# Who waits for the ring to come free: GpSimd itself instead of SyncE, in a graph kernel that gathers edges through a ring of buffers

## The reference, cut to what matters

```python
def _L0_gnn_ref(x, edge_index, edge_type, W_rel, W_root, bias):   # 3 layers, 8 edge types, D = 256
    src, dst = (edge_index[0], edge_index[1])
    for l in range(n_layers):
        xr = jnp.einsum('nd,rde->rne', x, W_rel[l])
        msg = xr[edge_type, src]
        agg = jax.ops.segment_sum(msg, dst, num_segments=x.shape[0])
        x = jax.nn.relu(agg + x @ W_root[l] + bias[l])
    return x

def _L1_gnn_ref(x, Wv, bv, wq, bq, wk, bk, src, dst):
    h = x @ Wv + bv
    q = h @ wq + bq
    k = h @ wk + bk
    e = q[src] + k[dst]
    c = jnp.where(e > 0, e, NEG_SLOPE * e)
    m = jax.ops.segment_max(c, dst, num_segments=n)
    ex = jnp.exp(c - m[dst])
    s = jax.ops.segment_sum(ex, dst, num_segments=n)
    attn = ex / s[dst]
    msg = h[src] * attn[:, None]
    return jax.ops.segment_sum(msg, dst, num_segments=n)

h = jnp.maximum(_layernorm(x, axis=-1), 0.0)
x = x + _L0_gnn_ref(h, ...)
h = jnp.maximum(_layernorm(x, axis=-1), 0.0)
x = x + _L1_gnn_ref(h, ...)
```

## Time and profile before

| | us |
|---|---|
| median of 3 runs | 5318.29 |
| lowest and highest of them | 5300.09, 5330.71 |
| the profiled execution's own time | 5230.69 |
| its span, first to last instruction | 5229.0 |
| GpSimd busy | 3053.6 (58%) |
| TensorE busy | 3608.1 (69%) |
| ScalarE busy | 2196.4 (42%) |
| VectorE busy | 1656.7 (32%) |

### The profile page before, as it was taken

The page is one execution under the profiler, slowest core; times in us unless marked ns, Lnnn a source line. Parts: engine busy times, 40 slices in busy tenths (PEclk is TensorE's granted clock), DMA queues, the critical chain, the costliest instruction groups (busy, mean ns, idle before and its releaser), DMA issues.

```text
span 5229.0 us, 56297 instructions
## 1 busy us (share of the span) xinstructions
PE 3608.1 (69%) x12674; PEld 2495.8 (48%) x12674; DVE 1656.7 (32%) x4423; ACT 2196.4 (42%) x6033; POOL 3053.6 (58%) x3302
## 2 busy tenths in 40 slices
PE   9986787777874877777775554544554666666667
PEld 4444554555552554545553343433433555545555
DVE  4533343333331222212221111111112545445444
ACT  2232443334442443433442333333333666556665
POOL 1145666666654666666664666666664566556664
PEclk9997888889887988888887677767766888888888
DMA  6553555555553444444443333333332333333332
GB/s 215 194 197 125 185 185 173 180 185 183 183 178 110 132 138 129 134 130 140 131 136 101 97 104 102 102 103 104 103 101 76 96 101 102 94 88 101 100 98 76
DMA packets 240051, 681.47 MB, mean 130 GB/s; under 512 B 60188, under 2 KB 111988, under 8 KB 215028
## 3 DMA queue, kind: packets, MB, share of 16 engines
q0 software_dynamic: 152400, 419.03, 27.6%
q10 hardware_dynamic: 57240, 186.43, 9.6%
q1 hardware_dynamic: 30092, 72.34, 3.8%
HBM read 501.99 MB, written 175.58 MB: 130 GB/s over the span
## 4 chain that ended last, share of the span: by engine, by line
PE 41%; another core or an unknown queue 26%; issue 14%; ACT 12%; DVE 6%; ACTq 1%; DVEq 0%; DMA 0%; SPq 0%
PE bank L1549 16%; PE sum_ps L1635 13%; PE sum_ps L1762 5%; ACT masks L1454 4%; ACT masks L1360 3%; PE bank L1718 2%; PE bank L1712 2%; DVE root L812 2%; PE turn_ps L1534 1%; ACT wide L1431 1%; ACT masks L1368 1%; PE sum_ps L1628 1%; ACT stage L1470 1%; ACT stage L1267 1%
## 5 line engine op out<-in xcount | busy, mean ns | idle before, releaser
L594 POOL DMA_INDIRECT ring<-table,code x2361 | 2236.4, 947 | 1377.8 <-issue 730.6
L1635 PE MATMUL sum_ps<-ring,masks 128*128 x5292 | 1445.6, 429 | 310.9 <-issue 295.6
L1635 PEld LDWEIGHTS sum_ps<-ring,masks 128*128 128x128 f32 x5292 | 1134.0, 218 | 587.6 <-issue 407.5
L1549 PE MATMUL bank<-wide,xT 128*128 128x512 f32 (+1 forms) x2744 | 1123.8, 563 | 4.1 <-issue 2.7
L594 POOL DMA_INDIRECT ring<-h_table,code x787 | 744.9, 946 | 503.1 <-SPq L734 254.8
L1360 ACT ACTIVATE masks<-node_row,local 128x128 f32<-128x128 f32 x2646 | 788.0, 387 | 24.8 <-issue 10.8
L1549 PEld LDWEIGHTS bank<-wide,xT 128*128 128x128 f32 x2744 | 514.3, 190 | 560.0 <-issue 548.7
L1762 PE MATMUL sum_ps<-ring,stage 128*128 x1764 | 541.7, 459 | 235.4 <-ACT stage L1470 151.2
L1258 ACT ACTIVATE xT<-turn_ps 128x256 f32<-128x256 f32 x196 | 75.5, 385 | 1441.8 <-remote 594.4
L1762 PEld LDWEIGHTS sum_ps<-ring,stage 128*128 128x128 f32 x1764 | 390.8, 235 | 314.6 <-issue 256.6
L1267 ACT COPY stage<-bank 128x512 f32<-128x512 f32 x441 | 244.3, 584 | 695.6 <-remote 429.2
(11 more groups left out here) (218 smaller groups left out, 2328.3 us busy)
## 6 DMA issues: line engine op xcount, KB each, us to landing
table<-stage ACTq DMA_DIRECT2D x96, 1024.0 KB
back<-table ACTq DMA_DIRECT2D x49, 1024.0 KB
table<-stage SPq DMA_DIRECT2D x48, 1024.0 KB
ring<-table,code POOLq DMA_INDIRECT x2361
ring<-h_table,code POOLq DMA_INDIRECT x787
h_table<-stage ACTq DMA_DIRECT2D x49, 130.0 KB
back<-h_table ACTq DMA_DIRECT2D x49, 130.0 KB
features<-xT SPq DMA_DIRECT2D x49, 128.0 KB, 4.0
```

The costliest lines, as they stand in the source:

```text
L594: pool.indirect_dma_start(slot(c % RING, width), None, table, bass.IndirectOffsetOnAxis(ap=code[:, c:c + 1], axis=0)).then_inc(landed[n % ...
L1549: last = nc.tensor.matmul(bank[q][:, 0:width], xT[:, b, k, :], weights[:, k, 512 * q:512 * q + width], start=(k == 0), stop=(k == K - 1))
L1635: last = nc.tensor.matmul(sum_ps[b][:, 0:D], masks[:, b, s, :], at_offset(slots[s]), start=(s == 0 and l > 0), stop=(s == SLOTS - 1))
```

## The change

GpSimd no longer waits for `released`. It loads the numbers of `need` itself, eight at a time, does the two register steps for each group, and waits for `added` with that value. SyncE only waits for landed groups and counts them in `in_order`. The semaphore `released` and the constants `LAG` and `RELEASES` are gone. What GpSimd waits for is the same count of pieces as before, for the same group, ten before the one that it fills.

```diff
-    LAG = 8
-    RELEASES = GROUPS - RINGS
-    BATCH = 16
+    BATCH = 8
-        released = sem("released")
             def gather_pass(l, table, width):
                 if l:
                     pool.wait_ge(in_order, l * GROUPS)
+                counts = []
                 for n in range(GROUPS):
-                    if n >= RINGS:
-                        pool.wait_ge(released, l * RELEASES + n - RINGS + 1)
+                    m = n - RINGS
+                    if m >= 0:
+                        if m % BATCH == 0:
+                            end = min(m + BATCH, GROUPS)
+                            _, counts = nc.values_load_multi_w_load_instructions(
+                                need[0:1, m:end], engines=[pool.engine], min_val=1, max_val=NT * PIECES,
+                                skip_runtime_bounds_check_because="counts of pieces, largest over the tiles")
+                        value = (counts[m % BATCH] & AT_MOST_PIECES) + (CREDIT + l * NT * PIECES)
+                        settle(pool, value)
+                        pool.wait_ge(added, value)
                     for c in chunks_of(n):
                         pool.indirect_dma_start(
             def relay(l):
-                counts = []
                 for n in range(GROUPS):
                     sp.wait_ge(landed[n % RINGS], 16 * gathers_to(l, n))
                     sp.sem_inc(in_order, 1)
-                    m = n - LAG
-                    if 0 <= m < RELEASES:
-                        if m % BATCH == 0:
-                            end = min(m + BATCH, GROUPS)
-                            _, counts = nc.values_load_multi_w_load_instructions(
-                                need[0:1, m:end], engines=[sp.engine], min_val=1, max_val=NT * PIECES,
-                                skip_runtime_bounds_check_because="counts of pieces, largest over the tiles")
-                        value = (counts[m % BATCH] & AT_MOST_PIECES) + (CREDIT + l * NT * PIECES)
-                        settle(sp, value)
-                        sp.wait_ge(added, value)
-                        sp.sem_inc(released, 1)
```

More of the change, by code:

```diff
@@ L71, in gnn_program @@
     assert PIECES == -(-SLOTS // GROUP)
-    assert (SLOTS + GROUP - 2) // GROUP + 1 <= LAG < RINGS and PIECES >= 3
+    assert (SLOTS + GROUP - 2) // GROUP + 1 < RINGS and PIECES >= 3
     assert 1 < KM and FIRST_BLOCKS * P <= 512
```

## The result

| | before | after |
|---|---|---|
| median, us | 5309.19 | 5442.13 |
| lowest and highest, us | 5242.52, 5330.71 | 5437.61, 5444.87 |
| profiled execution, us (span) | 5230.69 (5229.0) | 5439.88 (5438.2) |

The changed kernel is slower: 1.0324 times the kernel before, 95% interval 1.028 to 1.0367. The medians are 133 us apart and the two profiled executions 209 us, because the profiled execution of the kernel before is shorter than all four runs behind its median.

A forecast was written before the change was run, and what follows sets the result against it. The prediction took GpSimd's own gather pace, 1.25 us each, plus ring stalls ended by TensorE's count, as the bound. Its terms, -8 + 0 + 0 + 0 + 0 = -8 us, gave 5318 - 8 = 5310 us, range 5235 to 5405.

The forecast's parts named there:

- The median: Whole kernel: the time before, 5318 us, on which the forecast laid its sum to reach 5310 us.
- One hop less: Ring stalls on GpSimd: without SyncE's step each ends sooner, 0.028 x 282 = 8 us gained, at most 73 us.
- Landing order and `in_order` sooner: SyncE's queue: releases no longer behind landings, landed counts no longer behind piece waits; 0 each, at most some 5 and 2.3 us.
- Loads and steps: GpSimd's queue: 166 us of loads and 55 us of register steps, hidden behind gathers or inside stalls, costed at 0.
- Rival A: GpSimd's loads and steps stand bare outside stalls: 137 us slower, 5455 us; all 221 us, 5539, if stalls don't shrink; chance 0.13.
- B: GpSimd in the passes: only long loads stick out past the gathers, 75 us slower, 5393 us; chance 0.11.
- C: GpSimd's ring stalls end sooner, the whole 0.26 us of each of 282 going: 73 us faster, 5245 us; chance 0.17.
- Gathers 1.25 us apart across loads: Sign of being right: GpSimd's gathers still start each 1.25 us across loads and steps.
- Time at the ring near 814 us: Sign of being right: GpSimd's ring wait stays near 814 us, now charged to TensorE's sums.
- Pass windows within 10 us: Sign of being right: the windows of the four passes stay within 10 us of before.
- The last sentence on what would make it wrong: Ring stalls: if their count arrives at another point of the gathers, everything forecast is small beside a large number.

The follow-up runs named there:

- e9: Kernel before, but GpSimd waits for `added` against constants, without relay, loads or registers; run at the slow level: 0.9994 of the kernel before.
- e5: The changed kernel once more, unaltered, beside the kernel before: 1.0294, attention pass 1404 us.
- e6: The kernel before, unaltered, run for a trace: passes of 1169, 1148, 1133 and 1227 us.
- e12: Changed kernel with SyncE's old loads, steps and waits for pieces back, counting on a semaphore nobody reads: 1.0283 of the kernel before.
- e1: Kernel before, but GpSimd waits for `added` against constants, without relay, loads or registers; run at the quick level: 0.9983 of the kernel before.
- e10: Kernel before with SyncE's relay, but GpSimd does loads and steps and waits for `released` at a register's value; slow level: 1.0343.
- e11: Kernel before with an unread semaphore's increment between GpSimd's wait for `released` and the gather, in all passes; slow level: 1.0409.
- e13: Kernel before with an unread semaphore's increment between GpSimd's wait and the gather, in the attention pass alone: 1.0333.
- e7: Changed kernel with 7 ring groups in place of 10: 1.0558 of the kernel before, attention pass 1581 us.
- e8: Kernel before with GpSimd waiting for `added` against constants, no relay, and 7 ring groups: 1.0429 of the kernel before, attention pass 1567 us.
- e3: Changed kernel with GpSimd also waiting for `in_order`, until the group two before has landed; quick level: 0.9994 of the kernel before.
- e4: Kernel before with an unread semaphore's increment between GpSimd's wait for `released` and the gather, in all passes; quick level: 1.002.
- e18: Kernel before with eight unread increments between GpSimd's wait and the gather, in the attention pass alone; quick level: 0.9997.
- e16: Kernel before with `RINGS` 11 in place of 10 and `LAG` 9 in place of 8: 1.0045, attention pass 1212 us.

## Why the prediction was wrong

- *The median* of before was 5309 us in the runs beside the changed kernel, and 5318 in the forecast's. That is not the error.
- *One hop less, -8 us.* The hop itself fits: SyncE's step is 0.024 us in the trace, and e9, which has it gone and the wait on the gather, is at 0.9994 (-3 us, with an interval of -10 to +3 us that can't tell 8 us from none). The failed step is the sentence that the 0.26 us "holds both SyncE's step and GpSimd's own start" and that "nearly all of it is GpSimd's own and stays". It took that start as given, whatever carries the wait. In the changed kernel the wait for `added` no longer rides on the gather, which carries `consts_ready` instead, and from count to start it takes 0.74 us in place of 0.28. The instruction order listed `added` beside the gather; only the trace shows the wait as a record of its own.
- *What a stall costs.* 61 + 73 + 51 + 101 = 286 stalls by 0.46 us are 132 us. The third pass has just that (51 x 0.46 = 23 us, measured 24). The first two have -13 and 8 us where 28 and 34 would be owed (12 and 18 us in e5 against e6), and the attention has 188 instead of 46 us. So the forecast put at nothing a term of some 130 us, and missed its fourfold size in one pass. In the table passes together the stalls do not pass on all of their 0.46 us: 19 us were measured there and 85 owed.
- *Landing order and `in_order` sooner, 0 and 0.* Right as far as the runs tell: e12 has them back and is as slow, e9 has neither and is as quick as before. The reason given for it was weak. That the wait of line 1633 never took over 0.727 us shows nothing, since e1 has records of 51 ns where TensorE waited up to 10.2 us. And the 2.3 us charged to line 723 rest on updates of `in_order` that the trace of the kernel before mostly lacks: it has 279 of them, e1 has 789.
- *Loads and steps, 221 us hidden.* Hidden was right, by the plain gap of 0.305 us and by e10 beside e11. The size of the loads was not: 96 by 0.566 us are 54 us, not 166. The steps are 52 us, near the 55. The nearest row, GpSimd's load of seven at 1.734 us, was a poor guide, and SyncE's 0.061 us per number the better one (0.071 here). The Trainium skill, Runtime: NRT & Kernel Launch, section Instruction fetch mechanics, has some 200 ns for each register, an estimate of 1.6 us for eight; this trace, with its 0.566 us, doesn't agree.
- *Rival A* gave 5455 us, near the 5442 measured, by a mechanism that does not act: gathers did not wait for loads and steps. That its time is near is luck. It named the gather behind a wait on a register's value as the suspect, and that is the gather that starts late; whether the register's value is the reason is not shown. It had chance 0.13. *B* and *C* did not occur: no load stuck out, and the mean stall over 0.4 us grew in every pass, from 2.74, 2.60, 3.25 and 2.67 us to 3.27, 2.78, 3.69 and 4.40 us. The first pass still got 13 us shorter, with 61 stalls in place of 81.
- *Signs.* Gathers 1.25 us apart across loads: seen. Time at the ring near 814 us: 1021. Pass windows within 10 us: one of four. The last sentence on what would make it wrong, a count that arrives at another point of the gathers, has something for it in the attention pass: the distances between its stalls changed from eight gathers to four and twelve. That this makes the loss is not shown. In e13 half of the distances (54 of 108) are still eight, with a loss of 184 us, and in e7 and e8 77 are, with passes of 1581 and 1567 us.

Not settled: by what chain the attention pass makes 185 us of 57. Known is that it needs only the later gather (e13), and that a ring of 7 lengthens the same pass and no other.

Not tested: whether a wait on a register's value could ride on the gather if nothing else did. The run for it is the changed kernel with the wait for `consts_ready` left out of `settle` once it has been met. If `added` then rides on the gather, the change should cost nothing, as e9 does.

Nor is it settled what makes the slow level, where the ring gets full. At the quick level VectorE's wait for a sum in the third layer ends with TensorE's record; at the slow level mostly nothing that the profile shows ends it. First e1, then the kernel before:

```profile
DVE stage L1061 <- PE sum_ps L1624: 770.6, 49, 29.4
```
```profile
DVE stage L1072 <- remote: 854.4, 41, 75.3
```

It isn't TensorE's semaphore alone. The trace of e1 has 980 updates of `added` and 50335 of the ten `landed`, that of the kernel before 846 and 8170, for the same work. Whether updates come late and several at once there, or are only missing from the record, the traces don't tell. At the quick level the unaltered changed kernel wasn't run; e3, which is that kernel with one wait more, is at 0.9994.

No version beats both kernels by a margin that counts. The one with constants (e1, e9) is level with the kernel before (0.9983 and 0.9994), and holds for one input only.

## What to carry to other kernels

The pacemaker is the engine whose own pace sets the time, here GpSimd. Ask of each wait on its path which instruction will carry it, and look in the trace, since a listing of the program can show two waits at one gather. A wait with nothing beside or behind it rode on the gather here. One with a second wait beside it (from the helper of a register's value) or an instruction behind it stood alone, and the gather started 0.46 to 0.52 us later at every stall. A helper can add such a second wait unseen. The kernel before leaves the wait on a register's value to an engine with slack and hands the pacemaker a count that it can wait for as a constant, and that costs it nothing that can be measured against e9. And price a delay per stall in each pass by itself: the change takes 188 us from a pass with 101 stalls and 19 us from three with 185.

## What the runs showed of the hardware

- From the update of `added` to the start of an indirect gather on GpSimd: 0.26 us when the gather carries that wait (e9, 4451.256 to 4451.515), 0.28 us with SyncE's step between (before), 0.74 us when a semaphore instruction of its own has the wait (after), 0.80 us when SyncE's step and an increment come on top (e4, e13). Each further increment behind the wait adds 0.08 us (e18).
- In the traces of both kernels an instruction that isn't a semaphore instruction carries one wait at most (9215 such waits in each).
- The record of a wait need not hold the waiting: 51 ns in e1 for waits of up to 10.2 us, 17 ns on GpSimd after a stall of 9.24 us. SyncE's wait of the earlier trace rows does hold it, with 4.322 us.
- One kernel takes 4431 and 4435 us (medians) in some sets of runs and 5228 to 5309 us in others, and both on a chip with the same number. The passes of the kernel before and of e9, which is level with it, take 1132 to 1227 us at the slow level, those of e1 985 to 994 us at the quick one.
- GpSimd loads eight registers in 0.566 us (median of 96), SyncE sixteen in 0.971 us.
- A ring of 7, 10 or 11 groups gives the same table passes within some 15 us, if the wait rides on the gather (e8, before, e16).
